# Four reorderings in a fused attention and feed-forward kernel: token forms of step 0, homes of x parts, places of the scale rows, tiles of the last quad

## The reference

```
h   = layernorm(x);  kv = h @ W_to_kv.T;  c = kv @ W_compress.T        # 64 values per token
ch  = layernorm(c) * gamma + beta
q   = rope(ch @ W_q_comp.T);  k, v = split(ch @ W_kv_comp.T);  k = rope(k)
o   = softmax(causal(q @ k.T / 8)) @ v                                 # 1024 x 1024 per sequence
x1  = x + (o @ W_comp2lat.T) @ (W_to_kv + W_out_res.T) + b
y   = layernorm(x1)
hid = fwht(silu(y @ W1.T) * (y @ W3.T))                                # 2048 hidden values, Hadamard
out = x1 + hid @ W2.T
```

## Time and profile before

| | us |
|---|---|
| timed runs: median of 3 (lowest to highest) | 2283.01 (2281.13 to 2283.22) |
| the profiled execution: its own time | 2280.13 |
| span of its profile, first to last instruction | 2278.3 |
| busy in the span: PE / DVE / ACT / POOL | 2172.3 / 1437.6 / 1045.2 / 231.7 |
| main loop, product 0 of step 0 to the last down matmul | 112.9 to 2275 |

### The profile page before, as it was taken

The page is one execution under the profiler, slowest core; times in us unless marked ns, Lnnn a source line. Parts: engine busy times, 40 slices in busy tenths (PEclk is TensorE's granted clock), DMA queues, the critical chain, the costliest instruction groups (busy, mean ns, idle before and its releaser), DMA issues. The chain is left out here.

```text
span 2278.3 us, 28484 instructions
## 1 busy us (share of the span) xinstructions
PE 2172.3 (95%) x10676; PEld 1046.4 (46%) x10676; DVE 1437.6 (63%) x2742; ACT 1045.2 (46%) x1577; POOL 231.7 (10%) x212
## 2 busy tenths in 40 slices
PE   6768899999999999999999999999999999999999
PEld 3423444444444444444444444444444444444443
DVE  7876676766557575766656665575756666563333
ACT  6845455444543544435444445435444354442221
POOL 2344554000000000000000000000000000000000
PEclk8799999999999999999999999999999999999999
DMA  8434322332123322233123321233222331223221
GB/s 327 151 130 150 113 95 96 120 120 95 60 82 114 111 96 78 82 118 116 68 91 106 120 95 60 82 114 111 95 79 82 119 115 68 84 80 112 82 84 51
DMA packets 59561, 236.50 MB, mean 104 GB/s; under 512 B 6432, under 2 KB 6560, under 8 KB 54048
## 3 DMA queue, kind: packets, MB, share of 16 engines
q1 hardware_dynamic: 59424, 234.68, 29.6%
HBM read 194.81 MB, written 39.85 MB: 103 GB/s over the span
## 5 line engine op out<-in xcount | busy, mean ns | idle before, releaser
L772 PE MATMUL PF<-XF,WS 128*128 128x512 f16 x1792 | 683.8, 382 | 20.4 <-ACT PF L1144 12.6
L773 PE MATMUL PF<-XF,WS 128*128 128x512 f16 x1792 | 682.0, 381 | 0.0
L774 PE MATMUL PF<-XF,WS 128*128 128x512 f16 x1792 | 681.7, 380 | 0.0
L796 PE MATMUL PD<-W2S,H 128*128 128x512 f16 x1024 | 388.7, 380 | 2.0 <-DVE H L1759 2.0
L798 PE MATMUL PD<-W2S,H 128*128 128x512 f16 x1024 | 388.9, 380 | 0.0
L797 PE MATMUL PD<-W2S,H 128*128 128x512 f16 x1024 | 388.8, 380 | 0.0
L1155 ACT ACTIVATE SH<-PF,afs 128x512 f32<-128x512 f32 x256 | 175.9, 687 | 346.3 <-PE PF L774 345.3
L1751 DVE SCALAR_TENSOR_TENSOR SH<-PF,afs,SH 128x512 f32<-128x512 f32 x256 | 191.6, 749 | 144.8 <-ACT SH L1155 116.8
L772 PEld LDWEIGHTS PF<-XF,WS 128*128 128x128 f16 x1792 | 176.4, 98 | 231.7 <-issue 37.5
L774 PEld LDWEIGHTS PF<-XF,WS 128*128 128x128 f16 x1792 | 176.0, 98 | 213.2 <-issue 3.2
L1163 ACT ACTIVATE H<-SH 128x1024 f16<-128x1024 f32 x128 | 135.1, 1056 | 286.1 <-DVE SH L1751 286.1
(11 more groups left out here) (312 smaller groups left out, 2366.4 us busy)
## 6 DMA issues: line engine op xcount, KB each, us to landing
WS<-wscr SPq DMA_DIRECT2D x112, 896.0 KB, 4.6
W2S<-w2scr SPq DMA_DIRECT2D x30, 1024.0 KB, 4.8
xraw<-xT SPq DMA_DIRECT2D x58, 256.0 KB, 4.7
ring<-x SPq DMA_DIRECT2D x56, 256.0 KB, 4.3
wscr<-WS SPq DMA_DIRECT2D x16, 896.0 KB, 3.7
out<-ring SPq DMA_DIRECT2D x56, 256.0 KB, 4.5
XF<-w SPq DMA_DIRECT2D x16, 512.0 KB, 8.7
RAW<-w13t SPq DMA_DIRECT2D x16, 512.0 KB, 4.4
```

The costliest lines, as they stand in the source:

```text
L772: pe.matmul(bank, wh, th, start=i < 2 and j == 0, stop=False, skip_group_check=True)
L773: pe.matmul(bank, wh, tl, start=False, stop=False, skip_group_check=True)
L774: m = pe.matmul(bank, wl, th, start=False, stop=j == 1, skip_group_check=True)
L796: pe.matmul(PD[:, t % 2, :], th, wh, start=j == 0, stop=False)
```

## The change

1. **Start of step 0.** ScalarE makes the two weight forms of head tile 1 right after token form 0, and the token forms 1, 4, 2, 5 after `copy_b(0)`, form 6 after the first `silu`. VectorE makes its low part of the weight forms (`forms_low(1)`) after token form 3, the low parts in the order 0, 3, 1, 4, 2, 5, and form 6 (sum and low) in the loop, after `sum_c(0)` and `sum_e(0)`. `xf_no` follows that order.
2. **x parts.** For every even chunk (before: only the first) parts with even `k` go to the lower half of Kh and Kl and parts with odd `k` to the upper half, so `conv(a, k)` waits for `cproj(a, k - 2)` instead of `cproj(a, k - 1)`. Odd chunks keep one home.
3. **Scale rows.** `SCALE_AT` is a list. Head tile to place, before and after: 5: 19, 20; 7: 33, 32; 8: 40, 38; 9: 48, 44; 10: 54, 58; 11: 61, 62; 13: 75, 76; 14: 82, 83; 15: 90, 92; tiles 2, 3, 4, 6 and 12 keep 1, 5, 12, 26 and 68.
4. **Last quad.** The order of halves is 0, 2, 1, 3, 4, ...: both first halves of the first two token tiles come first. A first half waits for two head tiles of its quad (`v_lo` at `4 q + 2`), a second half for all four; this wait holds in every quad.

```diff
-SCALE_AT = {1: 2} | {7 * k + 5 + y_held(7 * k + 5): k + 3 for k in range(NH - 3)}
+SCALE_AT = dict(zip((1, 5, 12, 20, 26, 32, 38, 44, 58, 62, 68, 76, 83, 92), range(2, NH)))
...
-    return 7 * s + ((0, 2, 3, 1, 4, 5, 6)[i] if s == 0 else i) + 1
+    return 7 * s + ((0, 2, 4, 1, 3, 5, 6)[i] if s == 0 else i) + 1
...
-            b = slice(0, 512) if a == 0 and k % 2 == 0 else slice(512, 1024)
+            b = slice(0, 512) if a % 2 == 0 and k % 2 == 0 else slice(512, 1024)
...
+                w.wait_ge(v_lo, 4 * q + 2 * half + 2)
                 if t == 0 and half == 0:
-                    w.wait_ge(v_lo, 4 * q + 4)
...
-            for i in range(4 * NK - 1, 4 * NK + 16):
-                down(i)
+            for i in (-1, 0, 2, 1, 3, *range(4, 16)):
+                down(4 * NK + i)
...
-                    w.wait_ge(p_cp, tile_no(a, k) - 1)
+                    w.wait_ge(p_cp, tile_no(a, k) - (1 if a % 2 else 2))
...
             tokens_high(0, 0)
+            forms_high(1, 0)
+            forms_high(1, 1)
             xtrans1(1, 0)
             xtrans1(1, 1)
             tokens_high(0, 3)
             xtrans1(1, 2)
             xtrans1(1, 3)
-            tokens_high(0, 1)
-            tokens_high(0, 2)
-            tokens_high(0, 4)
-            tokens_high(0, 5)
-            tokens_high(0, 6)
-            forms_high(1, 0)
-            forms_high(1, 1)
...
                 copy_b(k)
+                if k == 0:
+                    for i in (1, 4, 2, 5):
+                        tokens_high(0, i)
...
                 silu(k, 0)
+                if k == 0:
+                    tokens_high(0, 6)
...
             tokens_low(0, 3)
+            forms_low(1)
             tokens_sum(0, 1)
             tokens_sum(0, 4)
             tokens_low(0, 1)
             tokens_sum(0, 2)
-            tokens_sum(0, 6)
+            tokens_low(0, 4)
             tokens_low(0, 2)
-            tokens_low(0, 4)
             tokens_low(0, 5)
-            tokens_low(0, 6)
-            forms_low(1)
...
                 sum_c(k)
+                if k == 0:
+                    tokens_sum(0, 6)
...
                 sum_e(k)
-                if first:
+                if k == 0 or first:
                     tokens_low(s, 6)
```

More of the change, by code:

```diff
@@ L51, in slots @@
     return [(c, z - ODD * c) for c in range(2) if 0 <= z - ODD * c < NSLOT]
-def y_held(f):
-    return any(slot - TILE0 in ((0, 8, 16, 24) if c else (6, 12, 18, 24)) for c, slot in slots(0, f))
-SCALE_AT = {1: 2} | {7 * k + 5 + y_held(7 * k + 5): k + 3 for k in range(NH - 3)}
+SCALE_AT = dict(zip((1, 5, 12, 20, 26, 32, 38, 44, 58, 62, 68, 76, 83, 92), range(2, NH)))
 SPLIT_AT = {9 + i: i for i in range(16)}
```

## The result

| | before | after |
|---|---|---|
| timed on one chip: median (lowest to highest, runs) | 2282.70 us (2279.76 to 2283.60, 6) | 2274.18 us (2273.55 to 2275.37, 6) |
| ratio after to before, 95% interval | | 0.9965 [0.9953, 0.9978] |
| the profiled execution: its own time / span | 2280.13 / 2278.3 us | 2274.68 / 2272.9 us |

The forecast was 2272.9 us, its own range 2270 to 2276. The medians differ by 8.5 us (by the interval 5.0 to 10.7) where 10.1 were forecast, and 2274.18 lies inside the forecast's own range; the two profiled executions differ by only 5.45. A line number of the kernel after is three lower than that of the same line before (L772 is now L769).

What follows compares the result with a forecast made beforehand. TensorE, busy 95% of the span, was taken as the bound, its idle time and slow clock as what could be won. Terms 2.7 + 1.9 + 1.7 + 3.8 = 10.1 us gave 2283.0 - 10.1 = 2272.9 us, range 2266.5 to 2278.5.

Steps and rivals of the forecast that it cites:

- rival (b): Step 0's gains come back as later waits; only tail and steps 1 to 6 pay: 5.3 us, 2277.7, chance 0.16.
- 1 start: Start of step 0: first x product of chunk 2 moves from 134.9 to 132.2, 2.7 us, ends 0 and 5.3.
- 2 homes: Even chunks: fourth x product's wait goes in steps 1 to 6, 1.5 us; chunk 2 gives 0.4; sum 1.9.
- 3 scale: Scale rows: bank Y waits go, 4.0, less 0.8 for scale 9 and 1.5 for clock: 1.7 us, ends 0 and 4.0.
- 4 tail: Last quad: the gap before 2252.46 goes, 2.1, and its low clock, 1.7: 3.8 us, ends 2.1 and 4.1.
- Gain: 134.9 - 132.2 = 2.7 us: Closing step of the start's working: chunk 2's first x product comes near 132.2, and that lead is the gain.
- new VectorE waits of over 2 us in step 0: Sign that the forecast is wrong, as would be the 5.6 us wait still standing.
- ScalarE would wait for no x load: Expected sign in step 0: the store goes out near 116, so the x load behind it is no longer late.
- the work hangs on TensorE's products and moves up with them: Argument against the rival that step 0 is bound by VectorE's and GpSimd's order and its gains return as waits.
- So 4.02 us go: Scale rows: four scale matmuls' waits for bank Y, 0.78 twice, 1.99 and 0.47 us, vanish at the new places.
- The stand of tile 9: Scale 9 at place 44 waits for GpSimd's diagonals: TensorE stands 3.3 us, net 0.8, plus 1.5 for low clock.
- the 2.9 us: Timed median of before, 2283.01, lies this far above its profiled execution, 2280.13; the forecast kept that offset.

Runs made afterwards that it cites:

- part 2 alone: The kernel before with only the two homes for x parts of every even chunk; 2275.89 us, ratio 0.9975.
- the run without GpSimd's half: The kernel before with only the new start, and head tile 1's low weight forms wholly on VectorE; 2277.65 us, ratio 0.9983.
- h_first: The kernel before with the second home only for chunk 2, the even chunk of step 0; 2280.32 us, ratio 0.9992.
- a_s9: The kernel after with scale tile 9 put back from place 44 to place 48; 2272.79 us, ratio 0.9961 to before.

## Why the prediction was right, and which of its terms were not

The sum came out, 10.1 us forecast and 8.5 measured, but not term by term, and that it came out is largely luck: two terms that brought nothing were made good by one that brought more than three times its forecast, part of it clock. By the two traces, which differ by 5.45 us, rival (b) had the better number: 5.3, the tail and steps 1 to 6. By the parts alone:

| part | forecast | measured alone, medians (by the interval) | what the rows give |
|---|---|---|---|
| 1 start | 2.7 | 0.0 (-1.8 to 2.1) | 2.6 at 132.3, 0.8 to 1.4 at product 7 |
| 2 homes | 1.9 | 6.2 (3.7 to 7.8) | 1.7 chunk 2, 2.1 later steps, the rest clock |
| 3 scale | 1.7 | -1.2 (-2.7 to 1.4) | tiles 14, 15: 2.8; tile 9: -3.7 to -4.2; tiles 5, 7, 8: 0 |
| 4 tail | 3.8 | 4.1 (1.8 to 5.9) | 3.8, of it 1.7 clock |
| sum | 10.1 | 9.1, whole change 8.5 | |

**Part 4 was right in each step.** No matmul waits before the last quad's second halves, the clock is full over 29 us, and the last product's shift goes from -1.6 to -5.4: 3.8 us. What the working did not say is that 1.7 of these are only there in an execution whose clock would have fallen. Together with part 2 that matters: in part 2 alone the clock did not fall in the last quad, and the 1.65 us must not be counted twice.

**Part 1: the rows near the forecast, the worth wrong.** GpSimd's low part began at 109.90 (109.7 forecast), the xnorm1 took 2.35 us, a hold of 1.8 where 2.1 was forecast, product 1 came at 120.70 for 119.9, product 2 at 124.38 for 123.5, and the first x product at 132.29 for 132.2. The last agreement is luck: the forecast had product 4 end near 129.5, at a low clock, while in the rows the clock is full behind 124.38 and product 4 is done at 128.3; VectorE then gave that back, with sum 6 at 2.25 us for 1.2, a wait of 0.52 for ScalarE before low 6, and 1.22 us for conv(2,0) instead of 0.7. The step that failed is the one behind it: "Gain: 134.9 - 132.2 = 2.7 us". It reads the gain of a part off the place where the reading stopped. Six microseconds later more than half of it is gone. GpSimd's diagonals and forms of head tile 2 began 2.7 us earlier than before, but ended no sooner, at 134.35 for 134.28, because beside VectorE's token sums and low parts they took longer (2.25, 3.48 and 1.73 us in the rows above). Before, VectorE's short scale operations (L1645 and after, L1642 in the kernel after; 17 in a row) began at 134.76, just behind them, and took 3.3 us. The rows of before:

```profile
126.85 1.88 POOL L1978 TENSOR_SCALAR WX<-cst_s,st 128x128 f32<-128x128 f32 x2
128.70 2.49 POOL L1990 TENSOR_TENSOR WX<-RAW,sc 128x512 f32<-128x512 f32 x2
...
133.56 0.72 POOL L1997 TENSOR_TENSOR WX<-WX 128x256 f32<-128x256 f32 x1
...
134.76 0.16 DVE L1645 TENSOR_SCALAR st<-st 128x24 f32<-128x24 f32 x1
...
139.38 0.50 PE L507 MATMUL XY<-Kh,Wc 128*128 128x512 f32 x1 [2.03 <-DVE Kl L1398]
```

Now they begin at 132.15, lie beside them, and take 4.7 (0.70 and 0.65 for two that took 0.16 and 0.18). The second x product stands behind them at 138.20 with 3.45 us of wait, 1.2 earlier than before instead of 2.6, and itself runs at a low clock, so that product 7 starts 1.29 us behind it and not 0.90 as before: 0.8 are left of the 2.6. This wait, which was 2.03 us, is the nearest thing to the forecast's own sign of being wrong, "new VectorE waits of over 2 us in step 0". What is left is then less than one fall of the clock (1.1 us after product 23), and at the end of step 0 nothing of it can be told in the times. Nor was it true that ScalarE would wait for no x load: at 135.12 it does, 1.24 us, for the third. The Trainium skill, SBUF — State Buffer, section "SBUF: two separate sides", has the two engines exclude each other on a shared port pair; the rows and the run without GpSimd's half agree with it (2.35 against 0.54 us). This was named as rival (b), "its gains come back as later waits", and for part 1 it is what happened. I had argued against it that the work hangs on TensorE's products and moves up with them; GpSimd's begins sooner but does not end sooner.

**Part 2: a term sized too small.** Steps 1 to 6 have 2.0 us in after, 2.1 and 2.2 in the kernels with the part alone, for the 1.5 that were read off the idle times; each such time understates the loss by up to the overlap of two matmuls, 0.17 us. In chunk 2 of step 0 I took 0.4 us; it was 1.7 in the rows of part 2 alone and of h_first, because the low part that waited for the common home stood ahead of hidden(0,0) on VectorE, and with it of the whole chain of head tile 0. In the kernel after only 0.6 of it show, from -0.8 to -1.4 at product 10. The rest of the 6.2 us is clock, which the term had at nothing, and the scatter of the runs.

**Part 3: the saving was counted where the wait is, not where its cause is.** "So 4.02 us go" failed for 1.56 of them. Tile 7 no longer waits, but tile 8, moved two places forward, now does, and Bank Y was not the only thing in its way: the row's copy needs `sc`, which GpSimd is still reading, and I had looked at the diagonals as GpSimd's only part in it. Tile 10's wait came back before the transposes at 289.06 (1.42 us). The 1.99 and 0.47 us did go. The stand of tile 9 was forecast at 3.3 us and is 3.12, at 248.11 with the clock at 0.50 behind it: the shift grows by 4.3 us at once and, with the 2.12 us and the 0.4 given back as forecast, is still 3.7 at product 49. So the clock took not 1.5 but nearly 3 us: the scale matmuls, one product and one down tile ran at half speed, fourteen matmuls and not ten. The term was -0.8 - 1.5 = -2.3; in the rows it is -3.7 to -4.2, and by a_s9 against after -1.4 in the median.

**The median above the profiled execution.** I let the 2.9 us stand. They are not a constant offset: the profiled execution of the kernel after stands 0.5 us above its median. That of before kept its clock behind products 9, 23 and 46, where others lost it, and lost it behind the wait at 267.24, where others kept it; that this makes up the 2.9 us is not shown.

## To carry to other kernels

Follow a moved start until the next three waits behind it have been read with the new times: what a change releases earlier on a helper engine will lie beside other work, and two engines that hold each other may end no sooner for having begun sooner. Before you count a wait as removed, list every tile that the waiting operation and the one behind it read or overwrite, not only the one that ended the wait. Of the idle time that you remove, count its length (and a modelled overlap on top of each short wait), and the slow clock behind it as a chance, once and not once per edit.

## What the runs showed of the hardware that was not expected

The granted clock fell to half behind a stall of 2.35 us in the traces of four kernels and not in those of three others with the same stall and the same matmuls before it; behind idle times of 2 to 4 us in step 0 it is the same. With starts of step 0 up to 1.9 us apart this is of the size of the spread of 2 to 8 us between executions of one kernel, and perhaps why two kernels that differ by tenths in their rows differ by 3 to 4.5 us in their medians; neither is shown. Beside GpSimd, VectorE's operations of 24 columns took longer too (0.70 and 0.65 us for 0.16 and 0.18), and so did GpSimd's beside VectorE: its two multiplications of 512 columns together took 2.49 us alone in the trace of before and 3.48 beside VectorE's token sum and low parts in the trace of after.
